# A fused cross-attention and MLP block: VectorE instead of TensorE transposes the normalised x, and four fc2 chunks move forward

## The reference

```
xq  = layer_norm(x) * qn_w + qn_b          ctx = layer_norm(context) * cn_w + cn_b
q   = xq @ q_w                             k, v = split(ctx @ kv_w)
a   = softmax(where(mask, -max, q k^T / 4))        (per batch and head, over 77 positions)
x1  = x + (a v) @ proj_w + proj_b
h   = layer_norm(x1) * n2_w + n2_b
out = x1 + gelu(h @ fc1_w + fc1_b) @ fc2_w + fc2_b         (hidden size 1024, exact gelu)
```

## Time and profile before

| | |
|---|---|
| median of 3 runs | 902.93 us (869.41 to 1092.31) |
| the profiled execution | 866.66 us, of which the span of the profile is 864.8 us |
| TensorE busy | 788.1 us, 91% |
| VectorE busy | 576.0 us, 67% |
| ScalarE busy | 556.9 us, 64% |
| GpSimd busy | 352.4 us, 41% |
| mean granted TensorE clock | 0.966 of full speed |

### The profile page before, as it was taken

The page is one execution under the profiler, slowest core; times in us unless marked ns, Lnnn a source line. Parts: engine busy times, 40 slices in busy tenths (PEclk is TensorE's granted clock), DMA queues, the critical chain, the costliest instruction groups (busy, mean ns, idle before and its releaser), DMA issues.

```text
span 864.8 us, 17043 instructions
## 1 busy us (share of the span) xinstructions
PE 788.1 (91%) x5637; PEld 637.1 (74%) x5637; DVE 576.0 (67%) x1238; ACT 556.9 (64%) x765; POOL 352.4 (41%) x312
## 2 busy tenths in 40 slices
PE   4428589999999999999999999999999999999998
PEld 3326477869687777869787787869787787869587
DVE  4432966858687776858687776858586776858241
ACT  2405666766767766776767767776767767676732
POOL 2000243443626243453627243452627243442634
PEclk9858689999999999999999999999999999999999
DMA  6492646749393856749394856749393856739100
GB/s 199 119 128 85 101 73 151 106 136 142 109 138 97 150 97 149 105 139 137 112 132 96 153 95 154 102 145 130 121 127 99 150 91 157 100 101 141 30 25 25
DMA packets 89447, 100.47 MB, mean 116 GB/s; under 512 B 9029, under 2 KB 63545, under 8 KB 89401
## 3 DMA queue, kind: packets, MB, share of 16 engines
q1 hardware_dynamic: 89088, 99.81, 61.1%
q10 hardware_dynamic: 328, 0.27, 0.2%
HBM read 69.22 MB, written 30.83 MB: 116 GB/s over the span
## 4 chain that ended last, share of the span: by engine, by line
PE 65%; POOL 8%; issue 5%; DMA 5%; ACT 4%; DVE 2%; SPq 0%; POOLq 0%; ACTq 0%; DVEq 0%
PE A L834 12%; POOL g_lo L433 8%; PE F L947 8%; PE ST L905 8%; PE F L834 7%; PE A L914 7%; PE F L948 7%; PE F L949 7%; DMA QM<-sd 3%; PE ST L887 2%; PE A L930 2%; ACT g_hi L535 2%; PE A L849 1%; PE A L842 1%; PE A L887 1%
## 5 line engine op out<-in xcount | busy, mean ns | idle before, releaser
L433 POOL TENSOR_TENSOR g_lo<-g_f,g_hi 128x512 fp32r<-128x512 f32 x128 | 178.3, 1397 | 178.9 <-ACT g_hi L535 163.3
L501 ACT ACTIVATE probs<-ST 78x512 f32<-78x512 f32 x256 | 137.6, 588 | 48.7 <-PE ST L905 45.7
L947 PE MATMUL F<-w_hi,g_hi 128*128 128x256 f32 x512 | 152.6, 298 | 0.7 <-POOL g_lo L433 0.7
L948 PE MATMUL F<-w_lo,g_hi 128*128 128x256 f32 x512 | 144.6, 282 | 0.0
L949 PE MATMUL F<-w_hi,g_lo 128*128 128x256 f32 x512 | 144.3, 282 | 0.0
L427 POOL TENSOR_TENSOR oT_lo<-g_f,oT_hi 128x512 fp32r<-128x512 f32 x32 | 41.2, 1287 | 234.5 <-ACT oT_hi L508 234.5
L533 ACT ACTIVATE g_f<-F,bias 128x512 f32<-128x512 f32 x128 | 88.1, 688 | 68.9 <-PE F L834 43.6
L834 PE MATMUL F<-xT_hi,w_hi 128*128 128x512 f32 x256 | 108.0, 422 | 11.5 <-ACT g_hi L535 9.8
L521 ACT ACTIVATE QM<-mask_u 77x2048 fp32r<-77x2048 uint8 x64 | 116.9, 1898 | 0.0
L947 PEld LDWEIGHTS F<-w_hi,g_hi 128*128 128x128 f32 x512 | 97.4, 190 | 19.5 <-issue 18.5
L905 PE MATMUL ST<-QM,KM 127*78 127x256 f32 x512 | 91.7, 293 | 20.7 <-DMA QM<-sd 15.8
(11 more groups left out here) (141 smaller groups left out, 1619.2 us busy)
## 6 DMA issues: line engine op xcount, KB each, us to landing
QM<-qd SPq DMA_DIRECT2D x48, 512.0 KB, 14.7
xa<-in_x SPq DMA_DIRECT2D x16, 512.0 KB, 4.0
qd<-q_hi SPq DMA_DIRECT2D x32, 256.0 KB, 2.1
qd<-q_lo SPq DMA_DIRECT2D x32, 256.0 KB, 2.1
xin<-in_x SPq DMA_DIRECT2D x16, 512.0 KB, 5.2
out<-xin SPq DMA_DIRECT2D x32, 256.0 KB, 5.9
QR<-qd SPq DMA_DIRECT2D x16, 480.0 KB, 5.3
KM<-kd SPq DMA_DIRECT2D x48, 156.0 KB, 6.8
```

What stands on the lines that cost most here:

```text
L433: pool.tensor_tensor(g_lo[:, k], g_f[k % 2][:], g_hi[:, k].bitcast(F32), ALU.subtract).then_inc(g_lo_done, 1)
L501: act.activation(probs[:, quad % NSLOT, 2 * (p % 2):2 * (p % 2) + 2], ST[p % 2][0:MX].rearrange("p (h n) -> p h n", n=N), ACT.Exp, scale=S ...
L947: pe.matmul(dst, g_hi[:, k, tok], w2_hi[:, k], start=(k == 0), stop=False)
L948: pe.matmul(dst, g_hi[:, k, tok], w2_lo[:, k], start=False, stop=False)
```

## The change

The eight transposes on TensorE are gone. A new VectorE function, `x_columns`, makes them as sixteen transposes: each takes 32 partitions of `xa` (256 elements in each partition: four token tiles, two chunks, 32 channels) and writes them, block by block of 32 by 32, into 32 partitions of a new view `xT` of o_tok's memory. Which partitions are read changes with every instruction. `x_columns(j+2)` stands in VectorE's stream behind `normalise_x(j+2)` and ahead of `g_high(j, 6)`. `xT_split` now reads `xT` in SBUF instead of the PSUM banks. On TensorE the fc2 chunks 2 and 3 move from behind scores 11 to the place behind cT, so that four chunks stand there, and the wait for `shiftT_done` between the transposes goes. SyncE's load of xa waits for `xT_done`, counted in sixteens.

```diff
+        xT = o_tok[:].rearrange("p q n e -> p (q n e)").rearrange("p (k n) -> p k n", k=KC)
...
-        XT = (A[3], A[1])
...
-                sp.wait_ge(xT_mm, KC * j)
+                sp.wait_ge(xT_done, 16 * j)
                 sp.dma_start(xa[:], x_rows(j)).then_inc(xa_loaded, 16)
...
+            def x_columns(j):
+
+                dve.wait_ge(xn_done, TT * (j + 1))
+                dve.wait_ge(hT_mm, least(KC * (j - 1)))
+                for c in range(P // 32):
+                    for r in range(P // 32):
+                        dve.transpose(xT[32 * c:32 * (c + 1)].rearrange("p k (t n) -> p t k n", n=P)[:, :, :, 32 * r:32 * (r + 1)],
+                                      xa[32 * r:32 * (r + 1)].rearrange("p t (k n) -> p t k n", n=P)[:, :, :, 32 * c:32 * (c + 1)]
+                                      ).then_inc(xT_done, 1)
+
             def xT_split(j, k):
-                dve.wait_ge(xT_mm, KC * j + k + 1)
-                dve.tensor_copy(xT_hi[:, k], XT[k][:]).then_inc(xT_hi_done, 1)
+                dve.wait_ge(xT_done, 16 * (j + 1))
+                dve.wait_ge(f1_mm, least(HC * (j - 1)))
+                dve.tensor_copy(xT_hi[:, k], xT[:, k]).then_inc(xT_hi_done, 1)
                 dve.wait_ge(xT_hi_done, KC * j + k + 1)
-                low(xT_lo[:, k], XT[k][:], xT_hi[:, k]).then_inc(xT_lo_done, 1)
+                low(xT_lo[:, k], xT[:, k], xT_hi[:, k]).then_inc(xT_lo_done, 1)
...
             normalise_x(0)
+            x_columns(0)
...
             normalise_x(1)
+            x_columns(1)
...
                     normalise_x(j + 2)
+                    x_columns(j + 2)
                 g_high(j, HC - 2)
                 g_high(j, HC - 1)
...
-            def xT(j, k):
-                pe.wait_ge(xn_done, TT * (j + 1))
-                for t in range(TT):
-                    last = pe.transpose(XT[k][:, t * P:(t + 1) * P], xa[:, t, k * P:(k + 1) * P], ident[:])
-                last.then_inc(xT_mm, 1)
...
-            xT(0, 0)
             pe.wait_ge(cT_lo_done, 1)
-            xT(0, 1)
...
                     cT(j + 1)
-                    xT(j + 1, 0)
-                    pe.wait_ge(shiftT_done, j + 1)
-                    xT(j + 1, 1)
                 if mlp:
-                    fc2(j - 1, 0, 0)
-                    fc2(j - 1, 0, 1)
+                    for k in range(4):
+                        fc2(j - 1, 0, k)
                 scores(j, 2)
...
                 scores(j, 11)
-                if mlp:
-                    fc2(j - 1, 0, 2)
-                    fc2(j - 1, 0, 3)
                 attend(j, 3)
```

More of the change, by code:

```diff
@@ L167, in xattn_block @@
         cT_lo_done = sem("cT_lo_done")
-        xT_mm = sem("xT_mm")
+        xT_done = sem("xT_done")
         xT_hi_done = sem("xT_hi_done")
```

## The result

The changed kernel takes 981.12 us (median of four runs, 978.80 to 987.19) against 869.41 and 870.00 us for the kernel before: ratio 1.129, 95% interval 1.120 to 1.138, so 13% slower. Two other runs of before, of 902.93 and 1092.31 us, were disturbed and are left out. The profiled execution has a span of 977.0 us. The forecast was 980 us.

A forecast was written before the change was run, and what follows sets the result against it. TensorE's own order was taken to bound the kernel, with about 1 us of rest a pair. 14 x (6.4 + 1.5) + 3.2 = 114 us on 866.66 us gave 980 us, range 935 to 1017.

The forecast's parts named there:

- What TensorE saves: TensorE loses transposes of 0.88 us a pair, 13 us at most; moved fc2 chunks cost the same 0.72 us anywhere.
- The price of the transposes: On VectorE, sixteen transposes a pair at 0.46 us each, between 0.36 with overlap and 0.48 without; 0.60 if slow.
- Who blocks whom: VectorE instructions reading two SBUF elements a cycle, casts and xT_lo, wait for GpSimd's whole instruction; transposes do not.
- The new start of a body: xT_split waits behind g_low 6, 7 and both additions; q_proj 7.1 us later, pair 6.4 us longer, TensorE resting 5.9.
- The clock: After TensorE's rest, some 3 us of its work runs slow and loses 1.5 us a pair; bounds nothing or 1.85.
- The start: x_columns(0) puts 7.4 us ahead of bv_in on VectorE, so k_proj(0) starts some 3 us later; 3.2 in the sum.
- Only the cast waits: Rival: in xT_split only the casts into xT_hi wait for GpSimd, xT_lo does not; 887 us, chance 0.20.
- nothing waits: Rival: no xT_split instruction waits for GpSimd, only k_proj is late, by 1.3 us; 878 us, chance 0.13.
- Transposes wait too: Rival: VectorE's SBUF-to-SBUF transposes also wait behind g_low, some 3 us a pair more; about 1020 us, chance 0.05.

The follow-up runs named there:

- e1: Kernel before with only fc2 chunks 2 and 3 moved from behind scores 11 to behind cT and xT; 866.47 us, ratio 0.9986.
- e9: e6 with GpSimd's add_fc2_b at the end of the body's normalisation and x_columns(0) in VectorE's rests at the start; 866.5 us, ratio 0.998.
- e12: e9 with the edits of e10 and e11, eleven transposes ahead of g_high, scores 0 and 1 behind cT and two fc2 chunks; 860.27 us, ratio 0.9927.
- e11: e10 plus a one-column exponential on ScalarE behind the last gelu, so the table loads early; 863.41 us, ratio 0.9965.
- e5: Changed kernel, but from pair 2 on xT_lo reads one operand from PSUM and only xT_hi from SBUF (values wrong); 900.64 us, ratio 1.042.
- e7: e2 with nine of the sixteen transposes ahead of g_high and seven behind cT_split; 925.32 us, ratio 1.066.
- e6: e7 with g_low 6 and 7 also waiting for xT_lo, and other TensorE work put ahead of q_proj; 874.95 us, ratio 1.009.
- e2: Changed kernel, but GpSimd's add_proj_b and add_fc2_b wait until xT_lo of both chunks is written; 910.53 us, ratio 1.050.
- e3: Kernel before plus the sixteen VectorE transposes, their output unread and TensorE's transposes kept; 912.02 us, ratio 1.053.
- e10: Kernel before with normalise_ctx and normalise_x ahead of the last four row maxima, and TensorE's maxima, shift, scores and fc2 chunks rearranged; 874.74 us, ratio 1.009.
- e4: Changed kernel, but each transpose reads the same 32 partitions that it writes (off-diagonal blocks wrong); 956.8 us, ratio 1.105.

## Why the prediction was right

The time (980 against 981), the direction and the mechanism were right. That the time is right to 1 us is luck: two terms were off by about 0.5 us a pair in opposite directions. Point by point:

- **What TensorE saves.** At most 13 us, and the fc2 chunks cost nothing: e1 shows the second. No run shows the 13 us: of the 0.88 us a pair, e9 kept about half, and e12 0.6 against e11.
- **The price of the transposes.** Taken 0.46, measured 0.466 us apart (436 ns each). Estimated 7.4 us a pair, 7.45 measured. So the 0.44 us for one, worked out from half the elements, was right, and with 0.03 us between there is no overlap at all; 0.46 was taken as a value between two cases and is near because the two cases lie near each other.
- **Who blocks whom.** The casts were shown by rows of before; that xT_lo would be held for its two SBUF inputs was inferred from what the held ones had in common, and e5 shows it. Transposes, with one SBUF input, are not held: sixteen took 7.45 us at even distances (0.463 to 0.470 us) while three g_low ran beside them, and 7.44 at the start, with GpSimd at rest. One reading was off: the 0.83 us by which GpSimd was late behind the four xa instructions is not a rest. The timeline of before has that g_low from 414.55 to 416.82, 2.27 us instead of 1.30, so it was held while xa was written; the conclusion, that it works the other way too, stands.
- **The new start of a body.** q_proj stands 18.03 us behind normalise_x's start, against 11.50 before, so 6.5 us later where 7.1 were forecast. The order of the turns was the one forecast, all four with a turn each. g_low 6 was 0.2 us sooner, and each GpSimd instruction behind a turn of VectorE ended 0.15 to 0.2 us sooner than its usual length has it (2.2 us behind VectorE's end, not 2.4, for the additions). TensorE rested 4.8 and 3.1 us there in turn, not 5.9.
- **The clock.** What is left of the 7.8 us a pair, after 6.5 - 0.7, is 2.0 us, where 1.5 were taken and 1.85 was the upper bound. The windows show it directly: from q_proj's start on, 5.31 and 3.19 us of work in turn run at half the clock, which loses 2.7 and 1.6 us, 2.1 on average; the prediction had 3 us of such work. This term was too small, and the term before it too large by 0.6 us; the sum of 7.9 against 7.8 owes its closeness to that. The row that it was taken from was also misread. The clock in the trace of before was at half from 86.4 us, ahead of the rest of 4.55 us that begins at 92.1, so that row shows what half the clock costs but not that this rest brought it down.
- **The start.** k_proj(0) begins at 26.91 instead of 23.03 us: 3.9 us, 3.2 forecast.
- **The rivals.** "Only the cast waits" is excluded by e5 and by the two xT_lo of 1.66 and 2.71 us, "nothing waits" by the same rows. "Transposes wait too" would have shown gaps among the sixteen, and there are none.

What stays open: who gets the next turn when both engines have something to run. The four xa instructions of normalise_x, which follow each other without a wait between them, kept a g_low out until all had ended; between the four of xT_split, which stand behind waits, GpSimd came in each time. That the waits make the difference was not tried by itself. Nor is it known why in some pairs the clock falls behind a rest of 1.4 us and in others does not.

## What to carry to other kernels

Moving work to an engine with idle time moves its operands too: before taking PSUM out of a VectorE instruction, look at what GpSimd has queued beside it, because here the float32 casts from SBUF to SBUF and the instructions with two SBUF inputs waited until the GpSimd instruction that was running had ended, be it one of 1.3 or of 2.4 us. If it can't be avoided, put long GpSimd instructions beside VectorE work that reads PSUM, or cut them in pieces, and check at which instruction the turn comes up next (e7 and e6 each only moved it). A bound engine's rest costs more than its length when the clock falls behind it.

## What the runs showed of the hardware

- TensorE rests 1.4 us before k_proj in nearly every steady pair of e2 and e3. Some of these pairs have no stretch at half the clock and last 50.2 (e2) and 50.3 us (e3), some have 3.4 us of it and last 51.0 and 51.7 us, some 6.8 us and 52.6 to 53.2 us. In the trace of before, a rest of 1.67 us at 835 us was not followed by any.
- A GpSimd instruction that is held by VectorE is recorded with its wait in it: g_low takes 1.27 to 1.31 us, but 2.27 beside the four xa instructions, and add_proj_b 2.79 us beside a held xT_lo and cast and 2.41 before. With normalise_x elsewhere (e10) no g_low is over 1.31 us. A chain of waits can show the same wait as a piece of its own (0.83 us "issue" in the earlier trace rows).
- VectorE transposes of 32x256 (float32) are 0.466 us apart where the 32 partitions change each time and 0.33 to 0.37 where they stay the same (e4).
- The unheld cast of 128x512 from SBUF to SBUF takes 0.42 to 0.43 us, against 0.68 from PSUM.
